# Reordering GpSimd's queue and four VectorE/ScalarE steps in the joint program of a two-layer Macaron kernel

## The chip, the cores and the metric

The kernel runs on one core of one Trainium2 chip. The metric is the device time of one execution in microseconds (us); lower is better. The core has five instruction queues that run side by side and meet only at semaphores: TensorE (PE in the profile; its weight loads are PEld), VectorE (DVE), ScalarE (ACT), GpSimd (POOL) and SyncE (SP). Each queue is strictly in order: an instruction that waits holds everything that stands behind it on its queue. The DMAs that a queue issues run beside it.

## The reference

The input is 4 x 1024 tokens of 128 numbers. Six residual blocks follow each other; the two mixtures in the middle are what the change touches:

```python
x = x + 0.5 * L0_ffn(layernorm(x))     # mixture of 8 experts, top 2, gelu, layer norm behind it
x = x + L0_attn(layernorm(x))          # state space
x = x + 0.5 * L0_ffn(layernorm(x))     # mixture, gelu     } one program in the kernel,
x = x + 0.5 * L1_ffn(layernorm(x))     # mixture, swiglu   } "the joint program"
x = x + L1_attn(layernorm(x))          # receptance
x = x + 0.5 * L1_ffn(layernorm(x))     # mixture, swiglu
```

A mixture normalises each token, finds its two best of 8 experts, runs it through both and adds the two results, weighted. The gelu kind normalises the sum once more (scale `ln_g`, shift `ln_b`) before it is added to x.

## The kernel before

**Layout.** x stays in SBUF as 32 groups of 128 tokens. A mixture is cut into four parts of 8, 12, 8 and 4 groups; a quad is four groups. The joint program holds both middle mixtures: parts 0 to 3 are the gelu one, parts 4 to 7 the swiglu one, on the same tokens. Part 4 of the second kind normalises x as part 0 of the first kind left it, part 5 waits for part 1, part 6 for part 2, and so on.

**How a part goes.** VectorE takes the means and variances (`stats`), GpSimd raises the variances to the power -1/2 (`power`), VectorE writes the normalised tokens (`normalise`), TensorE turns them and forms the router's products (`turn_tokens`, `logits`), VectorE finds the two experts (`route`) and each token's place in a table sorted by expert (`places`, `table`). GpSimd then scatters the groups to that table in HBM, one indirect DMA for each group and choice (`send`: 24 for part 5, with its 12 groups). The experts read the table by tiles of 128 rows; their results go to a second table, from which GpSimd gathers them back (`fetch(p, q)`: 8 indirect DMAs for quad q of part p). `gates` (VectorE) works out the two weights. `scale_lower` (ScalarE) scales the first gathered half, `combine` (VectorE) adds the second, and for gelu parts `norm` (VectorE), `final_power` (GpSimd) and `finish` (VectorE) are the layer norm behind it. `shift` (GpSimd) adds `ln_b`/2 to one quad of x, 128x512 elements.

**Tiles and iterations.** The joint program has 184 tiles, four to an iteration, 46 iterations. Part p begins at tile 0, 23, 54, 77, 92, 115, 146, 169. Tiles 0 to 91 are gelu, the others swiglu. Per tile TensorE runs `first_products` (L595) and then `second_products` (L606) of the tile two before it; ScalarE applies the nonlinearity (`nonlinear`, L694 or L698) and stores results (`store`, L704); VectorE copies the next iteration's expert weights (`fill`, L989), multiplies (swiglu only, L968) and moves finished results out of PSUM (`output`, L977 or L979). `store` of an output waits for that `output`, and ScalarE's next `nonlinear` stands behind it.

**Where the other steps stand.** Their order is written out by hand. TensorE, ScalarE and VectorE each have a dictionary `beside`: `11: {0: at(gates, 1)}` means that in iteration 11, behind tile 0's own work, the engine runs `gates(1)`. GpSimd has one list for the whole program, in which `send` and `fetch` are paced by `after=at_tile(...)`: they don't start before a certain tile is through `first_products`. `await_sets` holds a gather until the results that it needs are stored. SyncE loads the tokens of iteration i+2; the first load that reaches into part p waits until all of part p's scatters have landed (`sent[p]`).

**The places that the prediction's steps touch.** In iteration 27 VectorE runs, behind tile 1, `finish(2, 0)`, `finish(2, 1)`, `stats(6)`, `normalise(6)` and `route(6)`; TensorE runs, behind tile 1 of the same iteration, `turn_tokens(6, 0)`, `turn_tokens(6, 1)` and the logits of part 6, which wait for `normalise(6)`. `finish(2, *)` waits for `final_power(2, *)` and the sixth and seventh `shift`; `normalise(6)` waits for `power(6)`.

Of the kernel before, what the change touches and what calls it, by code (L numbers as in the profile page):

```python
# [36 lines left out]
PARTS = 4  # L37
# [273 lines left out]
def mixture(nc, name, kinds, x, res, ident, slots_x, slots_y, spare, begun=None, prefetch=(), block_diag=None, out=None, start=None):  # L311
# [19 lines left out]
    QUAD0 = [sum(QUADS[:p]) for p in range(NPARTS + 1)]  # L331
# [19 lines left out]
    with ExitStack() as ctx:  # L351
# [331 lines left out]
        def _(act):  # L683
# [83 lines left out]
            if not gelu:  # L767
# [3 lines left out]
                for j in range(BODY):  # L771
                    if by_act(j, kinds[0]):
                        fill(j, word, LAG + j)
            copy_set(0, 0)
            at = lambda f, *a: [lambda: f(*a)]
# [19 lines left out]
                                           17: {1: at(scale_lower, 1, 1)},  # L795
                                           18: {3: at(scale_lower, 1, 2)},
                                           22: {0: at(copy_tokens, 5, 0), 1: at(copy_tokens, 5, 1), 2: at(copy_tokens, 5, 2)},
                                           24: {0: at(scale_lower, 2, 0)},
                                           26: {0: at(scale_lower, 2, 1)},
                                           27: {1: at(copy_tokens, 6, 0) + at(copy_tokens, 6, 1)},  # L800
                                           29: {1: at(scale_lower, 3, 0)},
                                           32: {2: at(copy_tokens, 7, 0)},
# [23 lines left out]
        def _(dve):  # L826
# [277 lines left out]
            if gelu:  # L1104
                normalise(2)
                stats(3)
            at = lambda f, *a: [lambda: f(*a)]
# [34 lines left out]
                                           8: {0: at(places, 3), 2: at(table, 3)},  # L1142
                                           9: {2: at(combine, 0, 0), 3: at(norm, 0, 0)},
                                           10: {2: at(combine, 0, 1), 3: at(norm, 0, 1)},
                                           11: {0: at(gates, 1)},
                                           12: {0: at(finish, 0, 0), 1: at(finish, 0, 1)},
                                           13: {0: at(stats, 4), 3: at(normalise, 4)},
                                           15: {0: at(route, 4), 3: at(places, 4)},
                                           16: {0: at(combine, 1, 0), 1: at(norm, 1, 0)},
                                           17: {2: at(combine, 1, 1), 3: at(norm, 1, 1)},  # L1150
# [4 lines left out]
                                           22: {2: at(route, 5)},  # L1155
                                           23: {2: at(places, 5)},
                                           24: {0: at(table, 5), 1: at(combine, 2, 0), 2: at(norm, 2, 0)},
                                           26: {0: at(combine, 2, 1), 1: at(norm, 2, 1)},
                                           27: {0: at(gates, 3),
                                                1: at(finish, 2, 0) + at(finish, 2, 1) + at(stats, 6) + at(normalise, 6) + at(route, 6)},  # L1160
                                           28: {1: at(places, 6), 3: at(table, 6)},
# [39 lines left out]
        def _(pool):  # L1201
            def power(p):
                pool.wait_ge(var_ready, p + 1)
                pool.tensor_tensor(group(rstd, p), group(ve, p), res["neg_half"][:, 0:PART_GROUPS[p]], ALU.pow).then_inc(rstd_ready, 1)  # L1204

            def gate_power(p):
                pool.wait_ge(diff_ready, p + 1)
                pool.tensor_tensor(e2[p][:, :], base_of[KIND[p]][:, 0:PART_GROUPS[p]], diff[p][:, :], ALU.pow).then_inc(e2_ready, 1)

            shifts = Steps(pool, shifted, 0)  # L1210

            def shift():

                xt = x[:, shifts.n * SUB:(shifts.n + 1) * SUB, :]
                shifts.step(pool.tensor_tensor(xt, xt, res["post_b"][:, :].rearrange("p (a d) -> p a d", a=1).broadcast_to([P, SUB, D]), ALU.add))
                shifts.settle()

            def shift_if_left():

                if gelu and shifts.n < GROUPS // SUB:  # L1220
                    shift()

            def keep_pace(after, run):

                first, per_run = after
                tiles = min(first + int(per_run * run), NTILES)
                if tiles > 0:
                    pool.wait_ge(h_ready, 2 * SET + tiles)

            def send(p, groups=None, after=(0, 0)):  # L1230

                sent_here = 0
                pool.wait_ge(index_ready, p + 1)
                if begun:
                    pool.wait_ge(begun[f"slots_zeroed{p}"], 16)
                for g in groups or range(PART_GROUPS[p]):
                    for k in range(TOP):
                        n = g * TOP + k
                        if n % PACED == 0:
                            keep_pace(after, sent_here / RUN)  # L1240
                        sent_here += 1
                        if p == PARTS - 1 and n and n % RUN == 0:
                            shift_if_left()
                        pool.indirect_dma_start(slots_x[:, :], bass.IndirectOffsetOnAxis(index[p][:, k, g:g + 1], 0),  # L1244
                                                tokens[p][:, g, :], None).then_inc(sent[p], 16)

            def fetch(p, q, choices=range(TOP), after=(0, 0)):

                for n, k in enumerate(choices):
                    for g in range(q * SUB, (q + 1) * SUB):  # L1250
                        if g % PACED == 0:
                            keep_pace(after, n + g % RUN / RUN)
                        if p == 1 and not both and g % RUN == 0:
                            shift_if_left()
                        pool.indirect_dma_start(back[p][k][:, g, :], None, slots_y[0:(SLOT0[p] + PART_TILES[p]) * P, :],  # L1255
                                                bass.IndirectOffsetOnAxis(index[p][:, k, g:g + 1], 0)).then_inc(came[p][q][k], 16)

            def final_power(p, q):
                if KIND[p] == "gelu":
                    pool.wait_ge(var2, QUAD0[p] + q + 1)  # L1260
                    wide = slice(q * SUB, (q + 1) * SUB)
                    pool.tensor_tensor(rstd2[p][:, wide], ve2[p][:, wide], res["neg_half"][:, wide], ALU.pow).then_inc(rstd2_ready, 1)

            def await_landings():

                for p in ALL:
                    for q in range(QUADS[p]):
                        for k in range(TOP):
                            pool.wait_ge(came[p][q][k], 16 * SUB)

            def await_sets(sets):

                pool.wait_ge(stored[0], (sets + 1) // 2 * 16 + 16)
                pool.wait_ge(stored[1], sets // 2 * 16 + 16)
# [9 lines left out]
            at_tile = lambda n, rate=RATE: (n - BEHIND, rate)  # L1284
# [23 lines left out]
            if both:  # L1308
                fetch(1, 0, after=at_tile(58))
                fetch(1, 1, after=at_tile(63))  # L1310
                fetch(1, 2, after=at_tile(68))
                final_power(1, 0)
                final_power(1, 1)
                send(4, range(0, 4), after=at_tile(73))
                final_power(1, 2)
                send(4, range(4, 7), after=at_tile(78))
                power(5)
                send(4, range(7, 8), after=at_tile(82))
                gate_power(4)
                while shifts.n < QUAD0[PARTS]:  # L1320
                    shift()
                pool.wait_ge(combined, QUAD0[1])
                await_sets(-(-TILE0[3] // SET))
                fetch(2, 0, after=at_tile(84))
                fetch(2, 1, after=at_tile(91, 2))
                send(5, range(0, 5), after=at_tile(94, 2))
                final_power(2, 0)
                final_power(2, 1)
                send(5, range(5, 9), after=at_tile(100, 2))
                power(6)  # L1330
                send(5, range(9, 12), after=at_tile(105, 1))
                gate_power(5)
                await_sets(TILE0[4] // SET)
                fetch(3, 0, after=at_tile(106, 1))
                send(6, range(0, 6), after=at_tile(112, 3))
                final_power(3, 0)
                send(6, range(6, 8), after=at_tile(121, 3))
                gate_power(6)
                pool.wait_ge(combined, QUAD0[3])
                await_sets(-(-TILE0[5] // SET))  # L1340
                power(7)
                fetch(4, 0, after=at_tile(127, swiglu_rate))
                fetch(4, 1, after=at_tile(134, swiglu_rate))
                send(7, after=at_tile(143, swiglu_rate))
                gate_power(7)
                await_sets(-(-TILE0[6] // SET))
                for q in range(QUADS[5]):
                    fetch(5, q, after=at_tile(152 + 7 * q, swiglu_rate))
                pool.wait_ge(combined, QUAD0[5])
                await_sets(-(-TILE0[7] // SET))  # L1350
                fetch(6, 0, after=at_tile(175, swiglu_rate))
                fetch(6, 1, after=at_tile(182, swiglu_rate))
                pool.wait_ge(combined, QUAD0[4])
                await_sets(NTILES // SET)
                fetch(7, 0)
                await_landings()
                return
# [655 lines left out]
```

## Time and profile before

| | |
|---|---|
| median of 3 runs | 1259.85 us (1258.63 to 1262.43) |
| the profiled execution | 1264.09 us, of which the span is 1262.1 us and 2.0 us lie around it |
| busy share of the span | PE 79%, PEld 67%, DVE 70%, ACT 48%, POOL 59% |
| joint program, first to last tile on PE | 391 to 766 us of the span |
| mean granted clock of TensorE | 0.908 of 2.4 GHz |

Times in the rows are microseconds from the span's start unless marked ns. In a timeline row the first number is the start, the second the busy time, `x8` the number of instructions merged into the row, and the bracket says how long the engine was idle just before and what ended it; "issue" is time in which it waited for nothing that the profile shows. A queue's name with a q (SPq, ACTq) stands for its DMA instructions.

### The profile page before, as it was taken

The page shows a single profiled execution, that of the slowest core. Times are in us where ns is not written, and L with a number is a line of the kernel's source. Part 1 is how long each engine was busy: PE and PEld are TensorE (multiplying, and loading weights), DVE is VectorE, ACT ScalarE, POOL GpSimd, SP SyncE. Part 2 cuts the span into 40 slices and gives each one's busy share as a digit, 9 for nine tenths or more (in the row PEclk, how much of TensorE's full clock was granted, in tenths as well). Part 3 has the DMA queues.
Part 4 walks back from the last instruction along what each step waited for, and adds up shares of the span by engine and source line. Part 5 has one row for each costly group of instructions (what it writes and reads, how often), then busy time and mean ns, then how long its engine had stood idle before and what let it go on. Part 6 is the DMA issues. An engine that isn't in the chain of part 4 may idle for free. (4 is left out here: it accounts for less than half of the span.)

```text
span 1262.1 us, 27472 instructions
## 1 busy us (share of the span) xinstructions
PE 995.8 (79%) x6835; PEld 840.8 (67%) x6836; DVE 879.6 (70%) x3115; ACT 602.4 (48%) x1746; POOL 747.7 (59%) x721
## 2 busy tenths in 40 slices
PE   2599999566546999999678993798799875599992
PEld 2499999543246999989568993344254434499892
DVE  5655677577784658677857763689969977576763
ACT  0266777556413676665434552451445131245562
POOL 2777548730047775687677666366635643777565
PEclk9999999877857999999979997799989986699996
DMA  7644345200002342333233442000000000244353
GB/s 234 226 145 138 108 131 159 73 4 0 0 19 90 112 112 76 104 95 98 78 93 118 122 126 73 1 1 1 1 0 0 0 0 13 90 123 130 107 157 104
DMA packets 146194, 102.94 MB, mean 82 GB/s; under 512 B 16324, under 2 KB 134934, under 8 KB 146070
## 3 DMA queue, kind: packets, MB, share of 16 engines
q1 hardware_dynamic: 70530, 39.35, 10.7%
q0 software_dynamic: 16384, 33.59, 8.9%
q10 hardware_dynamic: 59156, 28.57, 7.8%
q8 instruction: 51, 0.84, 0.3%
q14 instruction: 73, 0.60, 0.2%
HBM read 52.44 MB, written 49.02 MB: 80 GB/s over the span
## 5 line engine op out<-in xcount | busy, mean ns | idle before, releaser
L595 PE MATMUL gelu_hb<-gelu_xsT,gelu_weights 128*128 128x128 f32 x2208 | 298.8, 280 | 0.0
L595 PEld LDWEIGHTS gelu_hb<-gelu_xsT,gelu_weights 128*128 128x128 f32 x2208 | 275.0, 196 | 0.4 <-issue 0.2
L694 ACT ACTIVATE gelu_hid<-gelu_hb,gelu_weights 128x128 f32<-128x128 f32 x736 | 210.7, 372 | 113.7 <-PE gelu_hb L595 94.9
L1244 POOL DMA_INDIRECT slots_x<-gelu_xn,gelu_index x192 | 192.5, 1003 | 76.9 <-issue 52.3
L606 PE MATMUL gelu_ob<-w,gelu_hid 128*128 x1472 | 196.9, 278 | 4.9 <-DVE gelu_ys L977 4.9
L606 PEld LDWEIGHTS gelu_ob<-w,gelu_hid 128*128 128x128 f32 x1472 | 181.5, 194 | 5.2 <-issue 5.2
L1255 POOL DMA_INDIRECT raw_s<-slots_y,gelu_index x128 | 125.7, 982 | 56.0 <-issue 33.9
L1924 POOL TENSOR_TENSOR rwkv_tw<-rwkv_tw,rwkv_qr 128x512 f32<-128x512 f32 x64 | 79.4, 1275 | 54.0 <-DVE rwkv_tw L1883 45.1
L989 DVE COPY gelu_weights<-w 128x516 f32 x184 | 83.0, 469 | 38.1 <-issue 26.6
L977 DVE TENSOR_TENSOR gelu_ys<-gelu_ob,bias 128x128 f32<-128x128 f32 x184 | 47.2, 287 | 83.4 <-PE gelu_ob L606 81.4
L595 PE MATMUL swiglu_hb<-swiglu_xsT,swiglu_weights 128*128 128x128 f32 x736 | 98.7, 278 | 0.0
L595 PEld LDWEIGHTS swiglu_hb<-swiglu_xsT,swiglu_weights 128*128 128x128 f32 x736 | 90.6, 194 | 0.2
L1244 POOL DMA_INDIRECT slots_x<-swiglu_xn,swiglu_index x64 | 63.2, 987 | 29.7 <-issue 16.8
L687 ACT COPY gelu_xsT<-gelu_turn 128x256 f32<-128x256 f32 x138 | 52.1, 378 | 56.4 <-PE gelu_turn L581 55.6
L1883 DVE TENSOR_TENSOR_SCAN rwkv_tw<-rwkv_qd,rwkv_carry,rwkv_bank_a 128x512 f32<-128x512 f32 x64 | 76.6, 1258 | 0.0
L1204 POOL TENSOR_TENSOR gelu_rstd<-gelu_ve,neg_half 128x8 f32<-128x8 f32 (+2 forms) x12 | 20.0, 1670 | 94.9 <-DVE gelu_ve L842 94.8
L581 PE MATMUL gelu_turn<-ident,gelu_xs 128*128 128x128 f32 x276 | 54.2, 279 | 22.4 <-issue 10.4
L606 PE MATMUL gelu_ob<-s,gelu_hid 128*128 x368 | 57.9, 281 | 16.3 <-DVE gelu_hid L968 16.3
L968 DVE TENSOR_TENSOR swiglu_hid<-swiglu_hid,swiglu_hb 128x256 f32<-128x256 f32 x92 | 38.4, 417 | 37.6 <-ACT swiglu_hid L698 37.2
L698 ACT ACTIVATE gelu_hid<-gelu_hb 128x256 f32<-128x256 f32 x92 | 35.2, 382 | 60.9 <-PE gelu_hb L595 50.7
L606 PEld LDWEIGHTS gelu_ob<-s,gelu_hid 128*128 128x128 f32 x368 | 48.8, 193 | 19.0 <-issue 18.9
L1707 PE MATMUL rwkv_bank_b<-rwkv_tw,sel 128*128 128x512 f32 x128 | 59.3, 598 | 2.1 <-POOL rwkv_tw L1924 1.6
(368 smaller groups left out, 2024.4 us busy)
## 6 DMA issues: line engine op xcount, KB each, us to landing
gelu_xs<-slots_x SPq DMA_DIRECT2D x69, 256.0 KB
slots_y<-gelu_ys ACTq DMA_DIRECT2D x138, 128.0 KB
swiglu_xs<-slots_x SPq DMA_DIRECT2D x23, 256.0 KB
slots_y<-swiglu_ys ACTq DMA_DIRECT2D x46, 128.0 KB
slots_x<-gelu_xn,gelu_index POOLq DMA_INDIRECT x192, 2.2
raw_s<-in_L_ffn_w ACTq DMA_DIRECT2D x12, 256.0 KB
slots_x<-zeros SPq DMA_DIRECT2D x2, 1472.0 KB, 9.7
w<-in_L_ffn_w SPq DMA_DIRECT2D x1, 2048.0 KB, 13.5
```

The lines of the kernel that those rows point to most:

```text
L581: last = pe.transpose(turn[:, j * P:(j + 1) * P], xs[:, odd * BODY + half * SET + j, :], ident[:, :])
L595: last = pe.matmul(hb[j][:, c * P:(c + 1) * P], weights[:, odd * BODY + j, c * P:(c + 1) * P], xsT[j // SET][:, j % SET, :], start=True, s ...
L606: last = pe.matmul(o, hid[:, r, c * P:(c + 1) * P], w2[:, bass.ds(e, 1), c, :].rearrange("p a d -> p (a d)"), start=c == 0, stop=c == CH[k ...
L687: act.copy(xsT[half][:, :, :], turn[:, 0:SET * P].rearrange("p (j d) -> p j d", j=SET)).then_inc(set_ready, 1)
L694: last = act.activation(hid[:, j % RING, c * P:(c + 1) * P], hb[j][:, c * P:(c + 1) * P], ACT.Gelu, bias=weights[:, odd * BODY + j, FF + c ...
L977: dve.tensor_tensor(y, o, res["bias"][:, bass.ds(es[n] * D, D)], ALU.add).then_inc(y_done, 1)
L989: dve.tensor_copy(weights[:, slot, 0:WIDTH[kind]], table_of[kind][:, bass.ds(e, 1), :].rearrange("p a f -> p (a f)"))\
L1244: pool.indirect_dma_start(slots_x[:, :], bass.IndirectOffsetOnAxis(index[p][:, k, g:g + 1], 0), tokens[p][:, g, :], None).then_inc(sent[p] ...
L1255: pool.indirect_dma_start(back[p][k][:, g, :], None, slots_y[0:(SLOT0[p] + PART_TILES[p]) * P, :], bass.IndirectOffsetOnAxis(index[p][:, k ...
L1707: pe.matmul(bank_b[b][:, :], res["sel"][:, j, :], T(b, 2), start=False, stop=j == HD - 1).then_inc(S["sum_done"], 1)
L1883: dve.tensor_tensor_scan(tw[b][:, j % 2, 1:TILE + 1], q["d"][b][:, :], bank_a[b][:, :], carry[b][:, j:j + 1], ALU.mult, ALU.add).then_inc( ...
L1924: pool.tensor_tensor(T(b, 2), tw[b][:, j % 2, 0:TILE], q["r"][b][:, :], ALU.mult).then_inc(S["m_done"], 1)
```

## The change

All of it lies in the joint program, and no instruction is added or dropped:

- GpSimd: the three last `shift`s stand between `fetch(2, 0)` and `fetch(2, 1)`, no longer ahead of `fetch(2, 0)`. `final_power(2, 0)` and `final_power(2, 1)` stand behind 18 of part 5's 24 scatters, no longer behind 10. The last 6 scatters stand ahead of `power(6)`, no longer behind it, and their pace is one tile less (104 for 105).
- VectorE: `gates(1)` goes from iteration 11 to 14; `combine(2, 1)` and `norm(2, 1)` go from iteration 26 to 25.
- ScalarE: `scale_lower(2, 1)` goes from iteration 26, tile 0, to iteration 24, tile 3.

```diff
@@ ScalarE's beside @@
-                                           24: {0: at(scale_lower, 2, 0)},
-                                           26: {0: at(scale_lower, 2, 1)},
+                                           24: {0: at(scale_lower, 2, 0), 3: at(scale_lower, 2, 1)},
@@ VectorE's beside @@
-                                           11: {0: at(gates, 1)},
                                            12: {0: at(finish, 0, 0), 1: at(finish, 0, 1)},
                                            13: {0: at(stats, 4), 3: at(normalise, 4)},
+                                           14: {0: at(gates, 1)},
                                            15: {0: at(route, 4), 3: at(places, 4)},
...
                                            24: {0: at(table, 5), 1: at(combine, 2, 0), 2: at(norm, 2, 0)},
-                                           26: {0: at(combine, 2, 1), 1: at(norm, 2, 1)},
+                                           25: {0: at(combine, 2, 1), 1: at(norm, 2, 1)},
@@ GpSimd's list @@
                 gate_power(4)
-                while shifts.n < QUAD0[PARTS]:
-                    shift()
                 pool.wait_ge(combined, QUAD0[1])
                 await_sets(-(-TILE0[3] // SET))
                 fetch(2, 0, after=at_tile(84))
+                while shifts.n < QUAD0[PARTS]:
+                    shift()
                 fetch(2, 1, after=at_tile(91, 2))
-                send(5, range(0, 5), after=at_tile(94, 2))
+                send(5, range(0, 9), after=at_tile(94, 2))
                 final_power(2, 0)
                 final_power(2, 1)
-                send(5, range(5, 9), after=at_tile(100, 2))
+                send(5, range(9, 12), after=at_tile(104, 1))
                 power(6)
-                send(5, range(9, 12), after=at_tile(105, 1))
                 gate_power(5)
                 await_sets(TILE0[4] // SET)
                 fetch(3, 0, after=at_tile(106, 1))
```

## Rows read from the trace of the kernel before

**Rows 1.** Windows: length, PE busy, granted clock, DMA share, GB/s.

```profile
492.00:495.00 3.00, 3.00 (x16) 0.50 0.30 87
...
567.00:573.60 6.60, 6.00 (x28) 0.50 0.32 99
...
634.70:645.30 10.60, 8.56 (x37) 0.50 0.19 65
```

**Rows 2.** Timeline of PE, tile 0 of iterations 11, 12 and 13.

```profile
480.20 1.06 PE L595 MATMUL gelu_hb<-gelu_xsT,gelu_weights 128*128 128x128 f32 x8
...
487.78 1.06 PE L595 MATMUL gelu_hb<-gelu_xsT,gelu_weights 128*128 128x128 f32 x8
491.26 1.60 PE L606 MATMUL gelu_ob<-w,gelu_hid 128*128 x8 [2.42 <-DVE gelu_ys L977]
...
499.67 1.06 PE L595 MATMUL gelu_hb<-gelu_xsT,gelu_weights 128*128 128x128 f32 x8
```

**Rows 3.** Timeline of DVE and POOL around the old `gates(1)`.

```profile
485.05 0.24 DVE L880 TENSOR_TENSOR gelu_weight<-gelu_first,gelu_e 128x96 f32<-128x96 f32 x1
...
486.14 4.08 POOL L1215 TENSOR_TENSOR x<-x,post_b 128x512 f32<-128x512 f32 x3
...
489.51 1.00 DVE L989 COPY gelu_weights<-w 128x516 f32 x1
```

**Rows 4.** Timeline of DVE and POOL in iteration 14.

```profile
511.21 0.57 DVE L977 TENSOR_TENSOR gelu_ys<-gelu_ob,bias 128x128 f32<-128x128 f32 x2 [0.64 <-PE gelu_ob L606]
...
511.62 1.03 POOL L1255 DMA_INDIRECT raw_s<-slots_y,gelu_index  x1 [5.83 <-DMA slots_y<-gelu_ys]
...
515.80 0.49 DVE L977 TENSOR_TENSOR gelu_ys<-gelu_ob,bias 128x128 f32<-128x128 f32 x2 [2.92 <-PE gelu_ob L606]
```

**Rows 5.** Timeline of DVE, first and last instruction of `gates(5)`, also 12 groups.

```profile
677.92 0.26 DVE L880 TENSOR_TENSOR gelu_weight<-gelu_first,gelu_e 128x96 f32<-128x96 f32 x1
...
679.99 0.35 DVE L898 TENSOR_REDUCE gelu_own<-gelu_picked 128x24 f32<-128x192 f32 x1
```

**Rows 6.** Timeline of `normalise(4)` and of iterations 20 to 22.

```profile
507.75 2.14 DVE L849 TENSOR_SCALAR gelu_xn<-x,gelu_mv,gelu_rstd 128x128 f32<-128x128 f32 x8
...
567.60 2.07 PE L606 MATMUL gelu_ob<-w,gelu_hid 128*128 x8 [2.45 <-DVE gelu_ys L977]
...
568.49 7.21 DVE L849 TENSOR_SCALAR gelu_xn<-x,gelu_mv,gelu_rstd 128x128 f32<-128x128 f32 x12
...
571.41 3.94 POOL L1215 TENSOR_TENSOR x<-x,post_b 128x512 f32<-128x512 f32 x3
...
588.75 0.26 DVE L860 COPY gelu_lg<-gelu_side 128x96 f32<-128x96 f32 x1 [5.60 <-PE gelu_side L565]
```

**Rows 7.** Timeline of POOL, iterations 23 to 27.

```profile
599.88 1.00 POOL L1244 DMA_INDIRECT slots_x<-gelu_xn,gelu_index  x1 [3.32 <-DVE gelu_index L937]
...
613.20 1.05 POOL L1262 TENSOR_TENSOR gelu_rstd<-gelu_ve,neg_half 128x4 f32<-128x4 f32 x1
620.36 1.33 POOL L1262 TENSOR_TENSOR gelu_rstd<-gelu_ve,neg_half 128x4 f32<-128x4 f32 x1 [6.11 <-DVE gelu_ve L1058]
621.59 1.02 POOL L1244 DMA_INDIRECT slots_x<-gelu_xn,gelu_index  x1
...
631.64 1.67 POOL L1204 TENSOR_TENSOR gelu_rstd<-gelu_ve,neg_half 128x8 f32<-128x8 f32 x1
...
640.99 2.30 POOL L1208 TENSOR_TENSOR gelu_e<-e_one,gelu_diff 128x12 f32<-128x12 f32 x1
```

**Rows 8.** Timeline of DVE and PE in iteration 27.

```profile
625.58 2.18 DVE L1075 SCALAR_TENSOR_TENSOR x<-raw_s,gelu_rstd,x 128x128 f32<-128x128 f32 x8
...
630.15 0.17 DVE L842 TENSOR_SCALAR gelu_ve<-gelu_mv 128x8 f32<-128x8 f32 x1
...
634.67 1.12 PE L557 MATMUL gelu_side<-ident,gelu_xn 128*128 128x128 f32 x4 [10.40 <-DVE gelu_xn L849]
...
645.26 0.48 PE L581 MATMUL gelu_turn<-ident,gelu_xs 128*128 128x128 f32 x2 [0.60 <-DMA gelu_xs<-slots_x]
```

## The prediction

> **What bounds the kernel now.** I read the list of waits of each engine over the joint program first, then the timelines at the longest waits of TensorE (PE), then windows for the granted clock. PE sets the pace here: where nothing holds it, an iteration takes 7.58 us (480.20 to 487.78) [rows 2]. Three places are longer for reasons that the change touches.
>
> *Iteration 12* takes 11.89 us (487.78 to 499.67), 4.31 more than ordinary: PE waits 2.42 us for an `output` of VectorE (DVE) [rows 2] and then runs at half clock for a stretch [rows 1]. DVE was late because `gates(1)` ran in iteration 11 from 485.05 to 489.51, 4.46 us, while three shifts of GpSimd (POOL) ran beside it [rows 3]. The same work for as many groups takes 2.42 us (677.92 to 680.34) in `gates(5)`, where no shift runs [rows 5].
>
> *Iterations 20 and 21*: PE waits 2.45 us for an `output` [rows 6], then works without a gap at half clock until 573.6 [rows 1]. At the same time `normalise(5)` takes 7.21 us for 12 instructions; 8 undisturbed ones take 2.14, so 12 would take 3.2. The 4.0 us more lie beside three shifts [rows 6].
>
> *Iteration 27*: PE stands 10.40 us for part 6's normalised tokens [rows 8]. They wait for `power(6)`, at 631.64 [rows 7]. Its input was there at 630.32 [rows 8], so two things come together: POOL's queue, which sat idle for 6.11 us ahead of `final_power(2, 1)` [rows 7], and DVE's chain. After the stand the clock is low until 645.3 [rows 1], and PE waits another 0.60 us for loaded tokens [rows 8], because SyncE's load stands until all of part 5's scatters have landed, and the last six are issued only after `power(6)`.
>
> **The change, part by part.** All sums are differences inside the profiled execution (1264.09 us, 4.2 above the median of the runs); I carry them over to the median unscaled.
>
> 1. *`gates(1)` out of iteration 11.* DVE reaches the `output` of tile 1 some 4.5 us earlier, at about 486, ahead of PE's need at about 488.7. The shifts stay where they are and can still hold two fills, each for a shift's length of 1.3 us, but those fills are wanted only in iteration 12's tiles 2 and 3. So the wait and the half clock behind it go: -4.3 us. Lower bound 2.4 (the wait alone), upper 6.0 (if in other executions the stretch at half clock is as long as the other one in rows 1, 6.6 us for 3.0, which is 1.8 us of work more).
>
> 2. *`gates(1)` into iteration 14.* It costs DVE 2.4 us [rows 5]; no shift is near. In that iteration DVE idles 0.64 and 2.92 us, 3.56 in sum [rows 4]. The first `output` is ready at most 1.8 us later than at 511.8, because 0.64 of the 2.42 us are idle time; behind it on ScalarE (ACT) stand its store, a copy of turned tokens and the nonlinear step of tile 3. The next `output` waits for PE until 515.8 as before, so by then DVE has caught up. Price 0. With the cover gone it is what iteration 11 shows, up to 4.3.
>
> 3. *The 4.3 us is passed on.* Part 1's gathers start at a stored result of PE's own pace (5.83 us idle, ended by that store) [rows 4], so POOL's whole queue moves with PE. In the following I keep the old clock times; all are 4.3 earlier.
>
> 4. *Shifts behind `fetch(2, 0)`.* The gathers start about 4 us earlier, the shifts run at about 581.9 to 585.8 (8 gathers behind 571.4, at the 1.3 us of a scatter in rows 7), `fetch(2, 1)` starts and ends where it did, as the sum of the queue is the same. POOL then idles 3.32 us for part 5's index [rows 7], so small slips are covered. `normalise(5)` becomes 4.0 us shorter, but PE wasn't waiting for it: it ran without a gap at half clock. Around the new place of the shifts DVE has one fill, and then idles 5.60 us for the logits [rows 6]. Price 0 on the path; bounds 0 and -3.3 (the whole loss to the half clock, half of 6.6 us).
>
> The row shows that a vector instruction with an SBUF source stands for as long as a shift runs (7.21 us for 12) [rows 6]. The Trainium skill ("SBUF — State Buffer", section "Who interferes with whom") says the pair of ports that VectorE and GpSimd share is locked for the whole instruction, and adds a thing that speaks against this edit: a VectorE copy or tensor_scalar in a two-port mode also keeps GpSimd from writing descriptors. By that rule `fetch(2, 0)`, which now meets the 12 instructions of `normalise(5)`, could be up to 3.2 us late, just within the 3.32 us of idle time; the trace of before, where gathers rarely meet a run of such instructions, doesn't show it. It goes into no sum.
>
> 5. *`combine(2, 1)`, `norm(2, 1)`, `scale_lower(2, 1)` earlier.* The values for `final_power(2, 1)` are there an iteration sooner than at 620.36, long before the 18th scatter, and the 6.11 us of idle time go [rows 7]. DVE has more to do in iteration 25 and less in 26; whatever PE loses in 25, it only arrives at the stand of iteration 27 a little later, which costs nothing as long as the stand is longer than that. Price 0, bounds -0.5 and +0.5.
>
> 6. *Where `power(6)` now comes.* From the first scatter of part 5 to `power(6)` POOL took 31.76 us (599.88 to 631.64): 10 scatters 13.32, two powers and the idle time, 8 scatters 10.05 [rows 7]. Now it is 24 scatters and two powers without the idle time: 13.32 + 10.05 + 7.48 (the last six, from 633.51 to 640.99) = 30.85, plus 2.4 for the powers and 0.4 for the steps between, 33.65 us. So `power(6)` starts at 633.5: +1.9 us. What DVE does meanwhile: the powers are out at about 626, when DVE comes to `finish(2, *)` (625.58), and its variances are there at about 630.7 [rows 8], 2.8 us ahead. So the queue of POOL, no longer DVE, ends the stand of PE, and the stand grows by 1.9 us. Bounds: 24 scatters at the 1.25 us of the last six are 30.0, which gives +1.0; with `gate_power(5)` now beside `normalise(6)`, one more stalled instruction of 1.3 us, +3.2.
>
> 7. *The load.* All scatters are out by 633.3 instead of 641.0, so the 0.60 us wait for tokens goes: -0.6. Behind it `fetch(3, 0)` starts some 6 us earlier; nothing waited for it.
>
> Sum: -4.3 + 0 + 0 + 0 + 1.9 - 0.6 = -3.0 us, in the profile's scale 1264.09 to 1261.1; the median goes from 1259.85 to 1256.9. Everything behind iteration 28 keeps its distances: PE, and what is tied to it, is 3 us earlier. What a measurement of this kernel can tell from no change is about 0.3%, 3.8 us: faster means below 1256.1, slower above 1263.6.
>
> **The rivals.**
>
> *A, the stall only moves (slower).* `gates(1)` in iteration 14 holds the `output` so long that ACT's store, and with it the nonlinear step of tile 3, comes late, and PE waits there as it did in 12. That decides once DVE's extra work passes 3.56 us. Against it: 2.42 us for the same work without a shift. For it: iteration 14 also has the turning of part 4's tokens on ACT. Then only items 6 and 7 are left: 1259.85 + 1.9 - 0.6 = 1261.2.
>
> *B, the clock gives back more.* The half-clock stretches behind the waits at 12 and 20 were 3.0 and 6.6 us long after equal waits of 2.42 and 2.45 us [rows 1, 2, 6], so what a wait costs varies. With DVE free 4 us sooner in iteration 21 and the load ready in 27, the stretches at 567 and 634 could be 3.4 us shorter each, 1.7 us of work each: 1256.9 - 3.4 = 1253.5.
>
> *C, POOL becomes the bound.* Gathers or scatters that meet more vector work, or a late index, put `power(6)` another 3 to 5 us back; each is paid in full at the stand of iteration 27. 1256.9 + 4 = 1260.9.
>
> **Chances.** My forecast 0.50 (own range 1255.5 to 1258.5; a quarter of it below 1256.1), B 0.26, A 0.13, C 0.11. Faster: 0.13 + 0.26 = 0.39; slower by over 0.3%: 0.03 of A and 0.03 of C, 0.06; the same 0.55. The range reaches to B on the one side and most of A and C on the other: 1253.0 to 1261.0.
>
> **What the new profile would show.** Iteration 12 at about 7.6 us without a wait for `gelu_ys`; no wait of PE in iteration 14; `normalise(5)` at 3.2 us; three shifts between two runs of 8 gathers; 18 scatters in a row, two powers, 6 scatters, `power(6)` some 33.6 us after the first; PE's stand in iteration 27 at about 12 us; no wait for `gelu_xs` behind it. The forecast is wrong if the wait of iteration 12 stays or comes back in 14, if POOL waits inside the 24 scatters, or if `power(6)` waits for DVE.

## The result, and the profile of the changed kernel

In 22 runs each, taken on the same chips, the kernel before has a median of 1263.0 us and the changed one 1259.8 us: ratio 0.9974, 95% interval 0.9964 to 0.9984, so 3.3 us less (2.0 to 4.5). It is close to the difference that was forecast (-3.0). It lies within the 0.3% that the prediction called indistinguishable from no change, but with this many runs the interval excludes zero. The time itself came out 2.9 us above the 1256.9 forecast because the kernel before measured 1263.0 in the comparison and not the 1259.85 of its first three runs. The profiled execution took 1259.63 us, 4.5 less than that of before.

Iteration 12 and the ones around it, PE's timeline of the changed kernel (start, duration, engine, line, operation, operands, count, idle time before):

```profile
485.79 1.06 PE L595 MATMUL gelu_hb<-gelu_xsT,gelu_weights 128*128 128x128 f32 x8
486.68 1.06 PE L606 MATMUL gelu_ob<-w,gelu_hid 128*128 x8
487.79 1.06 PE L595 MATMUL gelu_hb<-gelu_xsT,gelu_weights 128*128 128x128 f32 x8
488.69 1.06 PE L606 MATMUL gelu_ob<-w,gelu_hid 128*128 x8
...
495.38 1.06 PE L595 MATMUL gelu_hb<-gelu_xsT,gelu_weights 128*128 128x128 f32 x8
```

The wait of [rows 2] is gone and the iteration takes 7.59 us (487.79 to 495.38). Windows of PE (stretch, length, busy, instructions, granted clock, DMA share, GB/s):

```profile
492.00:495.00 3.00, 3.00 (x29) 1.00 0.08 22
563.00:567.00 4.00, 2.22 (x10) 0.53 0.23 68
...
625.00:633.00 8.00, 0.00 (x0) 0.50 0.11 43
634.70:645.30 10.60, 9.47 (x44) 0.51 0.30 82
```

In the 3 us from 492 on, PE runs 29 matmuls at its full clock of 2.4 GHz where [rows 1] show 16 at 1.2. In iteration 21 (563 to 570) and behind the stand of iteration 27 it is at half clock as before.

DVE's timeline: its `output` in iteration 11, a fill stretched by a shift, the moved `gates(1)` (first and last instruction) with the `output` behind it, `normalise(5)`, and the end of part 6's variances with `normalise(6)`:

```profile
485.37 0.48 DVE L976 TENSOR_TENSOR gelu_ys<-gelu_ob,bias 128x128 f32<-128x128 f32 x2
...
489.14 1.49 DVE L988 COPY gelu_weights<-w 128x516 f32 x1 [0.77 <-issue]
...
505.84 0.25 DVE L879 TENSOR_TENSOR gelu_weight<-gelu_first,gelu_e 128x96 f32<-128x96 f32 x1
...
507.86 0.35 DVE L897 TENSOR_REDUCE gelu_own<-gelu_picked 128x24 f32<-128x192 f32 x1
508.23 0.43 DVE L988 COPY gelu_weights<-w 128x516 f32 x1
508.57 0.52 DVE L976 TENSOR_TENSOR gelu_ys<-gelu_ob,bias 128x128 f32<-128x128 f32 x2
...
565.67 3.16 DVE L848 TENSOR_SCALAR gelu_xn<-x,gelu_mv,gelu_rstd 128x128 f32<-128x128 f32 x12
...
626.83 0.23 DVE L841 TENSOR_SCALAR gelu_ve<-gelu_mv 128x8 f32<-128x8 f32 x1
632.10 2.14 DVE L848 TENSOR_SCALAR gelu_xn<-x,gelu_mv,gelu_rstd 128x128 f32<-128x128 f32 x8 [5.04 <-POOL gelu_rstd L1203]
```

`gates(1)` takes 2.39 us in its new place (505.84 to 508.23, where the fill behind it starts). `normalise(5)` is down to 3.16 us from 7.21 [rows 6]. `normalise(6)` waits 5.04 us for POOL: its variances are there at 627.1 and POOL's `power(6)` comes only at 630.4. POOL's timeline:

```profile
509.04 1.10 POOL L1254 DMA_INDIRECT raw_s<-slots_y,gelu_index  x1 [7.59 <-DMA slots_y<-gelu_ys]
...
596.67 1.00 POOL L1243 DMA_INDIRECT slots_x<-gelu_xn,gelu_index  x1 [3.33 <-DVE gelu_index L936]
...
620.51 2.02 POOL L1261 TENSOR_TENSOR gelu_rstd<-gelu_ve,neg_half 128x4 f32<-128x4 f32 x2
622.72 1.05 POOL L1243 DMA_INDIRECT slots_x<-gelu_xn,gelu_index  x1 [0.19 <-issue]
...
630.39 1.67 POOL L1203 TENSOR_TENSOR gelu_rstd<-gelu_ve,neg_half 128x8 f32<-128x8 f32 x1
```

From first scatter to `power(6)`: 33.72 us (596.67 to 630.39), against 31.76 [rows 7]. And PE:

```profile
564.78 2.07 PE L606 MATMUL gelu_ob<-w,gelu_hid 128*128 x8 [2.72 <-DVE gelu_ys L976]
...
633.27 1.12 PE L557 MATMUL gelu_side<-ident,gelu_xn 128*128 128x128 f32 x4 [12.41 <-DVE gelu_xn L848]
...
643.05 0.64 PE L581 MATMUL gelu_turn<-ident,gelu_xs 128*128 128x128 f32 x2
643.48 1.85 PE L595 MATMUL gelu_hb<-gelu_xsT,gelu_weights 128*128 128x128 f32 x8
```

The stand is 12.41 us against 10.40 [rows 8]. The wait for loaded tokens is gone, but the matmuls of the tile behind it (the eight of the row at 643.48) take 1.85 us instead of 1.06: they still have the half clock that the wait had sat out before.

For the experiments I use lengths of iterations, from one "PE L595" row of a tile 0 to the next, in us (last column: from part 1's first gather back to the start of iteration 14):

```
kernel                      12     14     20     21   26+27  gather
before                    11.89  10.20   7.76  13.27  33.15   4.37
before, profiled again    10.85  10.20   7.79  12.05  32.95   4.29
changed                    7.58  10.20   8.72  13.14  35.01   6.08
changed, profiled again    7.58  10.19   7.77  12.00  34.38   4.34
gates only                 7.58  10.19   8.71  13.36  32.98   5.73
scatters only             10.39  10.20   8.71  12.99  34.96   5.83
shifts only               12.30  10.20   8.72  12.25  32.91   5.67
all but gates             10.73  10.20   8.11  10.62  34.23   5.71
shifts of 11 later         7.76  10.20  11.77  12.26  33.83   5.81
gates thrice               7.58  13.97   7.77  11.92  34.07   5.73
power(6) behind 20         7.58  10.20   8.71  12.26  31.79   5.76
finish in 26               7.58  10.20   7.76  10.38  30.32   4.34
normalise first            7.58  10.20   8.11  12.13  27.87   5.71
```

### The profile page after: what moved, and what is told of

Read it like the earlier page. It is cut to its first block and busy times, and to the rows that moved or that the text cites. A ratio compares the mean times of both kernels' runs of the same rounds, so it can differ in the third digit from the quotient of the medians.

```text
span 1257.7 us, 27472 instructions
## 1 busy us (share of the span) xinstructions
PE 993.6 (79%) x6835; PEld 839.4 (67%) x6836; DVE 877.4 (70%) x3115; ACT 602.3 (48%) x1746; POOL 746.6 (59%) x721
## 5 line engine op out<-in xcount | busy, mean ns | idle before, releaser
L595 PE MATMUL gelu_hb<-gelu_xsT,gelu_weights 128*128 128x128 f32 x2208 | 297.9, 279 | 1.0 <-issue 1.0
L595 PEld LDWEIGHTS gelu_hb<-gelu_xsT,gelu_weights 128*128 128x128 f32 x2208 | 274.3, 196 | 1.2 <-issue 1.2
L595 PE MATMUL swiglu_hb<-swiglu_xsT,swiglu_weights 128*128 128x128 f32 x736 | 99.2, 279 | 0.0
L595 PEld LDWEIGHTS swiglu_hb<-swiglu_xsT,swiglu_weights 128*128 128x128 f32 x736 | 91.1, 195 | 0.2
```

Of the source, the lines that this page charges most:

```text
L595: last = pe.matmul(hb[j][:, c * P:(c + 1) * P], weights[:, odd * BODY + j, c * P:(c + 1) * P], xsT[j // SET][:, j % SET, :], start=True, s ...
```

## The experiments

All ratios are to the kernel before, run on the same chip beside the experiment; a thousandth is 1.26 us.

**1. The three parts, each alone.** `gates(1)` moved from `11: {0: ...}` to `14: {0: ...}` and nothing else:

> Of the change only gates(1) is moved from iteration 11 to 14; POOL's queue is that of before. My account: iteration 12 takes 7.6 us instead of 11.9, iteration 14 stays at 10.2, of the 4.3 us some 3 arrive at part 5's first scatter (the profile of after showed 3.2 there), power(6) stays 31.8 us behind it, so PE's stand in iteration 27 stays at 10.4: the time falls by 3 to 4.3 us, ratio 0.9966 to 0.9976, more than the whole change gave. Rival one, the whole gain is passed on: -4.3 or more, 0.9966 or below. Rival two, the gain of the whole change came from the shifts or from the clock and not from gates(1): no difference, 0.999 to 1.001.

Ratio 0.9973 (0.9959 to 0.9988), -3.4 us. Iteration 12 at 7.58 us, PE's stand as before, and the load wait too:

```profile
631.95 1.12 PE L557 MATMUL gelu_side<-ident,gelu_xn 128*128 128x128 f32 x4 [10.41 <-DVE gelu_xn L849]
...
642.41 0.44 PE L581 MATMUL gelu_turn<-ident,gelu_xs 128*128 128x128 f32 x2 [0.47 <-DMA gelu_xs<-slots_x]
```

This one line of the change gives as much as the whole change. The new order of part 5's scatters with the earlier `combine`, `norm` and `scale_lower` of (2, 1):

```
-    send(5, range(0, 5)); final_power(2, 0); final_power(2, 1)
-    send(5, range(5, 9)); power(6); send(5, range(9, 12))
+    send(5, range(0, 9)); final_power(2, 0); final_power(2, 1)
+    send(5, range(9, 12)); power(6)
```

(Here and in the other cuts of GpSimd's list the `after=` arguments are left out.)

> Of the change only POOL's order in part 5 (final powers behind 18 scatters, power(6) behind 24) and the earlier combine, norm and scale_lower of (2, 1); gates(1) and the shifts are where they were before. My account: power(6) comes 33.7 us behind the first scatter instead of 31.8, PE's stand grows from 10.4 to 12.4, the load wait of 0.6 goes, iteration 28 starts 1.3 to 2 us later: ratio 1.001 to 1.0016. Rival, the stand is set by DVE's variances as before and the last six scatters come early enough to pay: -0.6 us or 0, 0.9995 to 1.000.

Ratio 1.0013 (0.9995 to 1.0030): the middle, +1.6 us, is as expected, but the interval does not exclude 0. The profile shows the mechanism: with `gates(1)` and the shifts as before, `power(6)` comes 33.72 us behind the first scatter and PE stands 12.40 us.

```profile
599.52 1.00 POOL L1243 DMA_INDIRECT slots_x<-gelu_xn,gelu_index  x1 [2.58 <-DVE gelu_index L936]
...
633.24 1.67 POOL L1203 TENSOR_TENSOR gelu_rstd<-gelu_ve,neg_half 128x8 f32<-128x8 f32 x1
```

The shifts alone (`while shifts.n < QUAD0[PARTS]: shift()` put behind `fetch(2, 0)`):

> Of the change only the three shifts behind fetch(2, 0). My account: normalise(5) shrinks from 7.2 to 3.2 us, PE's iteration 21 stays at 13.1 to 13.3, fetch(2, 0) starts about 4 us earlier and fetch(2, 1) where it did; ratio 0.9995 to 1.0005. Rival (B of the prediction), DVE free 4 us sooner shortens the stretch at half clock: up to -3.3 us, 0.9974. Rival the other way: gathers beside normalise(5) stand until it is through, so index and scatters slip and power(6) with them, +1 to +3 us.

Ratio 0.9993 (0.9979 to 1.0008), -0.9 us: nothing that the clocked times can show. `normalise(5)` took 3.15 us, and PE waited in iteration 21 all the same:

```profile
571.64 1.17 PE L606 MATMUL gelu_ob<-w,gelu_hid 128*128 x8 [2.71 <-DVE gelu_ys L977]
```

And everything but `gates(1)`:

> The changed kernel with gates(1) back in iteration 11: all of the change but that. My account: iteration 12 has its stall again (10.4 to 12.3 us), PE's stand in iteration 27 is some 1.8 us longer than before, the shifts give nothing or up to 1 us through iteration 21: ratio to before 1.000 to 1.0015, so gates(1) alone carries the gain of the change. Rival: the shifts and the shorter normalise(5) carry part of it, 0.998 to 0.999.

Ratio 0.9995 (0.9981 to 1.0009). The shifts and the scatters together come to nothing that the clocked times can show. The middle lies between the first account (1.000 to 1.0015) and the rival's (0.998 to 0.999), and the interval reaches into both, so this run doesn't decide between them. Iteration 12 has the stall again (10.73 us).

**2. Is it `gates(1)` or the shifts beside it?** The kernel before, with the three shifts of iteration 11 behind `fetch(1, 0)` and `gates(1)` where it was:

> The kernel before with gates(1) still in iteration 11, and instead the three shifts that ran beside it put behind fetch(1, 0). It asks which of the two made the stall of iteration 12. If it takes both, as the prediction held: gates(1) takes 2.4 us instead of 4.5, DVE reaches the output some 2 us earlier, PE's wait of 2.4 us falls to 0.4 or nothing, the clock doesn't fall, and iteration 12 takes 7.6 to 8.5 us: 3.4 to 4.3 us gained there. The shifts then stand beside DVE in iterations 14 and 15 and hold fetch(1, 1) back by 4 us; if POOL is not late there, the time falls by about 3, 0.9975. Rival: gates(1) alone is too long for iteration 11, the wait stays at about 2 us and the time at 0.999 to 1.001.

Ratio 0.9998 (0.9983 to 1.0014). In place, the expectation held: `gates(1)` took 2.39 us there (485.34 to 487.73) and iteration 12 only 7.76. So the stall needed both, and either can be taken away. But the 4 us came back in iteration 20 (11.77 us): POOL, 4.1 us of shifts later, gives `final_power(1, 2)` late (at 556.80), and `finish(1, 2)` of DVE, in front of an `output`, waits for it. The gathers of this profile were late too (5.81 in the table), but so were those of "gates only" (5.73), where iteration 20 took 8.71.

```profile
519.05 4.13 POOL L1215 TENSOR_TENSOR x<-x,post_b 128x512 f32<-128x512 f32 x3
...
557.87 1.14 DVE L1075 SCALAR_TENSOR_TENSOR x<-raw_s,gelu_rstd,x 128x128 f32<-128x128 f32 x4 [3.37 <-POOL gelu_rstd L1262]
...
560.18 1.15 PE L606 MATMUL gelu_ob<-w,gelu_hid 128*128 x8 [2.75 <-DVE gelu_ys L977]
```

I had written "if POOL is not late there"; it was.

**3. Where rival A decides.** The changed kernel, with the first seven steps of `gates(1)` done three times in iteration 14 (the values stay the same):

```
-    14: {0: at(gates, 1)},
+    14: {0: at(gates_again, 1) + at(gates_again, 1) + at(gates, 1)},
```

> The changed kernel with the first seven steps of gates(1) done two more times in iteration 14 (the values stay the same): DVE has 3.1 us more there, 5.5 us in sum. By rival A of the prediction, which said that it decides past 3.56 us of extra work, the stall comes back in iterations 14 or 15: PE waits 1 to 2 us for an output, the clock falls, +2 to +4.3 us against the changed kernel, ratio to before 1.0000 to 1.001. My reading of the changed kernel's trace: the output that gates(1) holds back, at 508.6, is wanted only by iteration 15's first tile at about 514, so 5.5 us are still covered and nothing shows: ratio as of the changed kernel, 0.996 to 0.9985.

Ratio 0.9999 (0.9984 to 1.0014): the whole gain is gone. The expectation's own reading of the trace was wrong, rival A's was right. PE's and ScalarE's (ACT) timelines:

```profile
514.47 3.06 PE L565 MATMUL gelu_side<-laT,gelu_xT 128*128 128x8 f32 x16 [2.19 <-ACT gelu_xT L719]
...
517.84 1.92 PE L595 MATMUL gelu_hb<-gelu_xsT,gelu_weights 128*128 128x128 f32 x8
```

```profile
513.35 0.39 ACTq L704 DMA_DIRECT2D slots_y<-gelu_ys  x1
513.83 0.58 ACT L719 COPY gelu_xT<-gelu_side 128x512 f32<-128x512 f32 x1 [3.37 <-DVE gelu_ys L994]
```

PE did not stand for the late `output` (512.81) itself. The `output`'s store is in ACT's queue, ACT waits 3.37 us for it, and behind it stands the copy of part 4's turned tokens that PE's logits need. With 2.4 us of extra work nothing shows. With 5.7 us (506.76 to 512.46) iterations 14 and 15 take 13.97 and 9.97 us instead of 10.20 and 8.03, 5.7 more; from 515.0 to 517.8 PE's granted clock is 0.51. The clocked loss against the changed kernel is smaller, 3.2 us by the two ratios: later iterations of this profile are shorter than in the changed kernel's first one (20 and 21 by 2.2 us, 26 and 27 by 0.9). The limit lies between 2.4 and 5.7; the 3.56 us that the prediction took for it was not tried more closely.

**4. What ends the stand of iteration 27.** The changed kernel with `power(6)` four scatters earlier:

```
-    send(5, range(9, 12)); power(6)
+    send(5, range(9, 10)); power(6); send(5, range(10, 12))
```

> The changed kernel with one thing else: power(6) is issued behind 20 of part 5's scatters instead of 24, the last four behind it. My account, that POOL's queue ends PE's stand in iteration 27: POOL is through with the 20 by 3.4 us behind the powers (622.7 + 2.8 in the trace of after), waits for DVE's variances (there at 627.1), so power(6) comes 3.3 us earlier and then DVE, not POOL, sets the end; the stand is 9.1 us instead of 12.4, the last scatter lands early enough, 3.3 us less than the changed kernel, 5 to 6.6 less than before, ratio 0.9950 to 0.9965. Rival: the load of part 5's tokens, which needs the last scatters, takes over and gives back half or more: ratio 0.996 to 0.9975.

Ratio 0.9947 (0.9929 to 0.9966), its middle a little below the 0.9950 to 0.9965 expected. Iterations 26 and 27 are 3.2 us shorter than in the changed kernel, for 3.3 expected; POOL now waits for DVE, and the load does not take over.

```profile
626.35 1.67 POOL L1203 TENSOR_TENSOR gelu_rstd<-gelu_ve,neg_half 128x8 f32<-128x8 f32 x1 [2.04 <-DVE gelu_ve L841]
...
629.38 1.12 PE L557 MATMUL gelu_side<-ident,gelu_xn 128*128 128x128 f32 x4 [9.25 <-DVE gelu_xn L848]
```

**5. A faster version.** With DVE's share moved too:

```
     # POOL, from the changed kernel
+    send(5, range(0, 7)); final_power(2, 0); final_power(2, 1)
+    send(5, range(7, 9)); power(6); send(5, range(9, 12))
     # DVE
+    26: {3: at(finish, 2, 0) + at(finish, 2, 1) + at(stats, 6)},
+    27: {0: at(gates, 3), 1: at(normalise, 6) + at(route, 6)},
```

(The lines that these replace are left out.)

> The changed kernel with DVE's share moved too: final powers behind 14 scatters, power(6) behind 18, and finish(2, *) and stats(6) behind tile 3 of iteration 26 instead of tile 1 of 27. My account: DVE's variances are there at about 623.3, power(6) runs at 623.3 instead of 630.4, PE's stand ends at 626.4 instead of 633.3; then the last scatters, out at 632.6, bound the load of part 5's tokens to about 636.9, where PE comes at 636.2, so 0.7 us come back as a wait: 6 us less than the changed kernel, 8 to 9.5 less than before, ratio 0.9925 to 0.994. Rival: PE's tiles of iterations 26 and 27 wait for DVE, which does 4.5 us of finish and stats ahead of their multiplies, and what the stand loses they take: no better than behind 20 scatters, 0.995 to 0.9965.

Ratio 0.9944 (0.9924 to 0.9964), above the expected 0.9925 to 0.994 and by clocked time not to be told from experiment 4. `power(6)` ran at 619.21, but iterations 26 and 27 were 4.7 us shorter than in the changed kernel and not 6: `normalise(6)` began at 623.10, 2.2 us behind `power(6)`'s end, with `gates(3)` and a multiply and an `output` ahead of it on DVE. The load wait that was expected did not come. The same with `normalise(6)` ahead of `gates(3)`:

> As the kernel with finish and stats(6) in iteration 26 (1254.6 us, 0.9944), with normalise(6) at tile 0 of iteration 27 and gates(3) behind it. There power(6) was through at 620.9 and normalise(6) began at 623.1, behind gates(3) and two vector instructions of DVE. My account: the stand ends 2.2 us earlier; the load of part 5's tokens, ready some 5.0 us behind the last scatter's start at 627.5, so at 632.5, then holds PE, which comes at 631.8, for 0.7 us: 1.5 us gained, ratio to before 0.9925 to 0.994. Rival: the load or POOL's queue bounds the place already, nothing gained: 0.9944 or above.

```profile
626.00 1.11 PE L557 MATMUL gelu_side<-ident,gelu_xn 128*128 128x128 f32 x4 [5.63 <-DVE gelu_xn L848]
...
636.40 0.44 PE L581 MATMUL gelu_turn<-ident,gelu_xs 128*128 128x128 f32 x2 [0.41 <-DMA gelu_xs<-slots_x]
```

Ratio 0.9934 (0.9921 to 0.9947), 1254.9 us beside 1263.0, from 6 runs: the lowest ratio of all, some 5 us below the changed kernel by the two ratios. Iterations 26 and 27 are 2.45 us shorter than in the version before it (1.5 were expected; the load wait is 0.41 and the tile behind it runs at full clock), 7.1 shorter than in the changed kernel; the clocked times don't separate it from that version or from that of experiment 4 (the intervals overlap). Of the three versions this is the only one whose interval lies wholly below the changed kernel's (0.9964 to 0.9984).

**6. The same two kernels, profiled again.** The unchanged kernels, once each, to know what a single profile is worth:

> The kernel before, unchanged, profiled once more, to see how much of a place's length is the execution's. In the profile of before part 1's first gather came 4.4 us behind the start of iteration 14, in six of the seven other kernels profiled with iteration 14 of the same length 5.7 to 6.1 us. If that is the execution's and not the edits', this profile too shows 5.7 or more, iteration 20 takes 8.7 us instead of 7.8, and the whole loss of 1 us that the changed kernel showed in iteration 20 is no property of the change. If it belongs to the kernel, 4.4 and 7.8 come again. Iteration 12 takes 10.4 to 12.3 us, iteration 27 some 27.0.

> The changed kernel, unchanged, profiled once more. Iterations 12 and 14 at 7.6 and 10.2 us, the first gather of part 1 again 5.7 to 6.1 us behind iteration 14's start or, as the execution goes, 4.4; iteration 21 between 10.4 us (no stretch at half clock behind its wait) and 13.1; iterations 26 and 27 in sum 35.0, 1.9 us above before. If iteration 21 were the kernel's, 13.1 comes again.

For the kernel before, the account that such lengths are the execution's failed (4.29 us and 7.79 came again). But the changed kernel shows both: 6.08 and 8.72 in one execution, 4.34 and 7.77 in the other. Over thirteen profiles the gather came 4.3 to 4.4 us behind iteration 14's start in four, 5.7 to 6.1 in nine. Iteration 21 varies as well, behind the same wait: PE waited 2.46 us in each of the two profiles whose windows behind the wait follow. In the version with `finish` in 26 it ran at full clock there:

```profile
565.00:569.00 4.00, 4.00 (x39) 1.00 0.40 117
```

In the changed kernel's second profile, partly at half clock:

```profile
565.00:569.00 4.00, 4.00 (x27) 0.68 0.34 107
```

## Why the prediction was right, step by step

What was right is the difference, and its two large terms. The time itself, 1259.8 us, lies above the forecast's own range (1255.5 to 1258.5) and nearer to the times of rivals C (1260.9) and A (1261.2) than to 1256.9; only the comparison with 22 runs of the kernel before, and the profile, rule these out. That -3.0 meets -3.3 to a third of a microsecond is in part luck: the interval is 2.5 us wide, and term 7 gave nothing.

1. *`gates(1)` out of iteration 11, -4.3.* Right in place and size: 4.31 us in the first pair of profiles, 2.8 to 4.7 over the five profiles that keep the stall (10.39 to 12.30 against 7.58), inside the bounds of 2.4 to 6.0. Their average is 3.7, so the 4.3 of one profile was a little high. Experiment 2 shows the cause named: `gates(1)` stretched by shifts.

2. *Into iteration 14 for nothing.* Right: 10.20 us before and after. Experiment 3 shows that it is the cover that makes it free. The prediction named ACT's queue as the way; it is ACT's copy that is late first, not the nonlinear step that rival A put in front.

3. *The 4.3 us is passed on.* Right only in part. In the first pair of profiles POOL's gathers came 2.6 us earlier, not 4.3 (511.62 to 509.04), because the store ahead took longer to land: from its issue to the gather 4.98 us (504.06 to 509.04) against 3.26 (508.36 to 511.62). The single packets in the traces show why. The store's 128 KB are written between 1.6 and 2.7 us behind its issue. In the changed kernel's profile a 16 KB packet of a DMA queue of the kind "instruction" (q8) starts 2.57 us behind the issue and takes 0.96 us, and the store's last 8 KB are written only behind it, from 3.52 to 4.23. In the profile before, that packet starts at 3.25, when the store is through. So it is in all thirteen profiles: in the nine with the late gather the packet starts 2.2 to 2.6 us behind the store's issue and the store's last packet at 3.8 to 4.2; in the four others 3.2 to 3.8 and 2.6 to 2.7. The second profile of the changed kernel is one of the four, so the delay is no fixed price of the edit; both profiles of the kernel before are free of it, and what sets the packet's time stays open. The clocked -3.4 us of the gates alone is below 4.3, but its interval (1.5 to 5.2) holds both.

Iteration 20 was 0.96 us longer in the first profile of the changed kernel: PE waits 0.97 us there for nothing that the profile names. A packet of the other queue of that kind (q14) comes 4.2 us into iteration 20 in the five profiles where it takes 8.7 us, 3.6 us in the two with 8.1, and at most 3.3 us in the five with 7.8. That PE waits for its instructions there is an inference from this order; no experiment tested it.

4. *Shifts, 0.* `normalise(5)` at 3.16 us, `fetch(2, 0)` at 569.03, the idle time ahead of part 5's scatters 3.33 us against 3.32 [rows 7]: all as written. Shown: no loss, a gain of at most 2.7 us by the interval of the shifts alone. The 7.2 us of the old place are not fixed either: 7.00 in the second profile of the kernel before, but 4.75 to 4.76 in the three other kernels with the shifts there (gates only, scatters only, shifts of 11 later), where one of the shifts took 2.1 us instead of 1.3. Iterations 20 to 23 sum to 41.0 us on average in the four profiles with the old place of the shifts and to 40.1 in the eight with the new (the kernel with its stall in iteration 20 left out), so rival B's gain, if there is one, is nearer 1 us than 3.3.

The loss that the prediction weighed beside this step was not seen. The Trainium skill's rule ("SBUF — State Buffer", section "Who interferes with whom"), that a two-port VectorE operation keeps GpSimd from writing descriptors, doesn't show beside `normalise`. Over the thirteen profiles 30 scatters and gathers of the joint program ran behind another one with a `normalise` beside them and no fill; their median is 0.97 us, the longest took 1.00, and the 1535 with neither beside them have 0.96. No run shows whether `normalise` runs in a two-port mode. Beside fills there is a sign in the rule's direction: 25% of 643 took over 1.05 us (the longest 1.49), against 4% of the 1535. The first gather of `fetch(2, 0)` tells nothing of it. It met the end of `normalise(5)` in the version with `finish` in 26, came just behind it in the changed kernel, and as good as behind it, after the shifts, in the kernel before:

```profile
565.83 1.57 POOL L1255 DMA_INDIRECT raw_s<-slots_y,gelu_index  x1 [0.18 <-issue]
```

```profile
569.03 1.37 POOL L1254 DMA_INDIRECT raw_s<-slots_y,gelu_index  x1
```

```profile
575.64 1.63 POOL L1255 DMA_INDIRECT raw_s<-slots_y,gelu_index  x1 [0.28 <-POOL x L1215]
```

5. *`combine`, `norm`, `scale_lower` earlier, 0.* Right as a sum. PE lost 1.08 us in iteration 26 (7.19 against 6.11, a wait of 1.13 for `gelu_hid`), and it only came later to the stand.

6. *`power(6)`, +1.9.* Right: 33.72 us forecast as 33.65, the variances 3.3 us ahead of it where 2.8 was written, the stand 2.0 us longer; iterations 26 and 27 together +1.86. Between the averages of four profiles with this edit (both of the changed kernel, scatters only, all but gates) and four without (both of before, gates only, shifts only) it is +1.65, and +1.4 with the two kernels that stall elsewhere counted in (gates thrice, shifts of 11 later). The change's own core edit is thus a loss, and experiments 2 and 4 show that POOL's queue is what makes it.

7. *The load wait, -0.6.* This term was wrong in size: the wait went and nothing of it was gained. From the end of the stand to iteration 28 it takes 12.47 us in the profile before, with the wait, and 12.56 in that of the changed kernel, without it, where the tile that comes sooner runs at half clock (1.85 us at 643.48). The seven profiles without a wait there have 11.95 to 12.60, the six with one of 0.4 to 0.6 us 12.23 to 13.22. This is the one term of the sum that no run bears out. The range of the forecast covered it.

Sum of the steps as measured one at a time: -3.4 + 1.6 - 0.9 = -2.7 us, and the whole -3.3, forecast -3.0. Rivals: A is a real mechanism past the cover and did not act. B isn't decided: behind the wait of iteration 21 the half clock lasted 6.8 us in three of the five profiles with the old place of the shifts (3.4 and none in the others) and in one of the eight with the new (3.4 in five, none in two), which these few profiles can't tell from chance; in iteration 27 the half clock did not get shorter in the changed kernel. The 3.0 and 6.6 us that the prediction compared are lengths of the windows of [rows 1]; the stretches themselves lasted 3.4 and 6.8. C did not come, since inside the 24 scatters POOL never waited.

## What to carry to other kernels

When a change has several edits, price them one by one: here one moved line gave the gain, and the reordering that gave the change its name took nearly 2 us back. A queue's item that another engine stands for (`power(6)`) goes as far forward as its input allows, and the input is then moved forward too; each step was worth what the slack in the trace said (3.2 us for 3.3), until the next in line showed (4.7 for 6, for the vector work ahead of `normalise(6)`); these are lengths in one profile each, and only the last version's clocked interval lies wholly below the changed kernel's. When you take away a collision of two engines, move the one with slack: moving the shifts instead of `gates(1)` cured iteration 12 and made a stall of the same size in iteration 20.

## What the runs showed of the hardware

Behind a wait of 2.4 to 2.9 us PE ran on at full clock, or at half clock for 3.4 or for 6.8 us, at the same place and behind waits as long. Iteration 12, 7.6 us without the wait, took 10.4 to 10.9 us with the wait alone and 11.9 and 12.3 with 3.4 us at half clock. Iteration 21 took 10.4 and 10.6 with the wait alone, 11.9 to 12.3 with 3.4 us at half clock and 13.0 to 13.4 with 6.8; the second profile of the kernel before has 12.05 at full clock, with another wait of 1.5 us that the profile doesn't name. The wait can be forecast from a trace; what the clock adds only as a range of 0 to 3 us. I didn't find what decides it.

A short wait close to the end of a stretch at half clock can cost nothing: with 0.47 us of waiting for tokens (gates only) the stand's end and iteration 28 lay 12.29 us apart, without a wait 12.56 (changed).

One 128 KB store released its gather 3.2 to 3.3 or 4.6 to 5.0 us behind its issue. The long ones are those in which a 16 KB packet of an "instruction" queue started while the store was being written (2.2 to 2.6 us behind the issue) and the last 8 KB came behind it.

While three shifts ran on GpSimd, 12 vector instructions took 7.2 and 7.0 us, or 4.8 with one shift stretched to 2.1 us, instead of 3.2: the two engines hold each other up, in either direction.
